# Turning mixed attention values in 32x32 blocks on the vector engine, in a two-layer transformer kernel

## The reference

```python
attn = jax.nn.softmax(jnp.einsum('bnhd,bmhd->bhnm', q, k) * SCALE, axis=-1)
sa = jnp.einsum('bhnm,bmhd->bnhd', attn, v).reshape(Bx, Nx, C)
sa = sa @ sa_proj_w + sa_proj_b
```

## Time and profile before

| | |
|---|---|
| three runs | 1625.62, 1627.46, 1627.52 us (median 1627.46) |
| profiled execution, first to last instruction (the only time the profile gives for it) | 1627.8 us |
| PE, PEld busy | 91%, 79% |
| DVE busy | 69% |
| ACT, POOL busy | 59%, 44% |
| mean DMA rate | 30 GB/s |
| granted clock of PE, mean | 0.978 of full |

### The profile page before, as it was taken

One profiled execution on the slowest core, in us unless ns is written; L12 is line 12 of the kernel. 1 busy time (PEld: TensorE's weight loads), 2 busy tenths in 40 slices (PEclk: granted clock), 3 DMA queues, 4 the chain that ended last, 5 costly groups with the idle time before them and its releaser, 6 DMA issues.

```text
span 1627.8 us, 44574 instructions
## 1 busy us (share of the span) xinstructions
PE 1478.1 (91%) x17632; PEld 1288.7 (79%) x17632; DVE 1130.2 (69%) x2407; ACT 957.0 (59%) x1754; POOL 721.2 (44%) x982
## 2 busy tenths in 40 slices
PE   5989999999999999999998989889899897988987
PEld 4768888787888878788787877878778786887867
DVE  5556766666776766667777776866867777687664
ACT  3456565656656565666655655556655565655543
POOL 3133424333342434336557464464644636356321
PEclk9989999999999999999999999999999999999998
DMA  6110100101010010110112000000000001000000
GB/s 221 45 47 10 37 25 29 41 13 56 10 47 15 29 41 29 40 31 24 36 45 66 12 18 15 14 28 11 18 15 15 27 12 31 5 11 15 2 14 14
DMA packets 34251, 49.38 MB, mean 30 GB/s; under 512 B 3488, under 2 KB 24928, under 8 KB 34048
## 3 DMA queue, kind: packets, MB, share of 16 engines
q1 hardware_dynamic: 33760, 46.01, 9.0%
q10 hardware_dynamic: 288, 0.52, 0.1%
HBM read 38.08 MB, written 8.45 MB: 29 GB/s over the span
## 4 chain that ended last, share of the span: by engine, by line
PE 70%; DVE 16%; issue 7%; ACT 4%; POOL 2%; SPq 0%; DMA 0%; DVEq 0%; POOLq 0%; ACTq 0%
PE score_t L677 8%; PE score L656 8%; PE p_mix L719 7%; PE p_unit L746 6%; PE p_unit L550 5%; PE p_unit L551 5%; PE p_unit L552 5%; DVE neg_max L1120 4%; PE p_out L550 3%; PE p_out L552 3%; PE p_out L551 3%; PE p_mix L581 2%; DVE k_t L1110 2%; PE p_turn L736 2%; PE p_turn L729 2%
## 5 line engine op out<-in xcount | busy, mean ns | idle before, releaser
L1120 DVE TENSOR_REDUCE neg_max<-score 128x8 f32<-128x1024 f32 x224 | 274.1, 1224 | 121.0 <-PE score L656 105.5
L656 PE MATMUL score<-k_t,q_t 32*128 32x256 f32 x1792 | 252.3, 398 | 32.5 <-DVE q_less L1130 16.5
L677 PE MATMUL score_t<-q_less,k_t 32*128 32x128 f32 x3584 | 267.0, 288 | 1.0 <-ACT probs_t L980 0.7
L677 PEld LDWEIGHTS score_t<-q_less,k_t 32*128 32x128 f32 x3584 | 224.0, 191 | 13.1 <-issue 7.1
L980 ACT ACTIVATE probs_t<-score_t 128x1024 f32<-128x1024 f32 x168 | 172.1, 1025 | 94.3 <-PE score_t L677 82.3
L656 PEld LDWEIGHTS score<-k_t,q_t 32*128 32x128 f32 x1792 | 161.5, 186 | 70.3 <-issue 31.6
L899 ACT ACTIVATE xt<-p_mix,mod_now 128x128 f32<-128x128 f32 x384 | 154.4, 454 | 80.3 <-PE p_mix L581 61.5
L1324 POOL TENSOR_TENSOR xt_lo<-xt,xt_hi 128x256 fp32r<-128x256 f32 x128 | 95.8, 749 | 207.1 <-ACT xt_hi L904 206.3
L746 PE MATMUL p_unit<-w_out,heads_t 128*128 128x256 f32 x512 | 147.0, 410 | 15.0 <-ACT q_t L943 8.2
L550 PE MATMUL p_out<-w_hi,hid_lo 128*128 128x256 f32 x512 | 151.9, 297 | 5.0 <-issue 2.6
L1167 DVE TENSOR_TENSOR hid_lo<-hid,hid_hi 128x256 fp32r<-128x256 f32 x256 | 141.8, 554 | 8.8
(11 more groups left out here) (161 smaller groups left out, 4349.1 us busy)
## 6 DMA issues: line engine op xcount, KB each, us to landing
ctxt<-in_ctxT SPq DMA_DIRECT2D x16, 512.0 KB, 3.8
side<-gates SPq DMA_DIRECT2D x15, 512.0 KB, 4.6
x_new<-in_x SPq DMA_DIRECT2D x32, 128.0 KB, 2.1
x_mid<-xs SPq DMA_DIRECT2D x8, 512.0 KB, 3.3
x_new<-x_mid SPq DMA_DIRECT2D x32, 128.0 KB, 2.0
out<-xs SPq DMA_DIRECT2D x8, 512.0 KB, 3.2
k_t<-in_L_f_wT SPq DMA_DIRECT2D x2, 1024.0 KB, 5.6
probs_t<-in_L_xcond_fc_w SPq DMA_DIRECT2D x1, 1024.0 KB, 8.8
```

What stands on the lines that cost most here:

```text
L656: mm = pe.matmul(score_banks(b, h)[:, r % 2, t * 2 * N:(t + 1) * 2 * N].rearrange("p (e n) -> p e n", e=2), q_t[s][rows(r), t, tokens], k_ ...
L677: mm = pe.matmul(turned_banks(b, h)[:, r % 2, x * N:(x + 1) * N], k_t[s][rows(r), t, e, tokens], q_less[rows(r), j % 2, t, e, :], start=Tr ...
L1120: dve.tensor_reduce(by_half[:, 2 * h:2 * h + 2, 0:CT, :], score_banks(b, h)[:].rearrange("p r (t e n) -> p r t e n", t=CT, e=2), AX.X, ALU ...
```

## The change

The matmuls of mix_values write their 128 tokens as four runs of 32 columns into p_mix, so that p_mix holds, for each 32 tokens, the four slots side by side (mix_by_slot). DVE transposes p_mix in 32x32 blocks into SBUF (mix_blocks), takes the reciprocal there, scales out of SBUF into head_blocks, and transposes those in blocks into heads_t. turn_heads, turn_back, move_mix and move_heads and their semaphores go. turn_blocks (transpose and reciprocal) stands in step 7, right behind scale_heads in DVE's order; scale_heads (product and second transpose) in step 8. The release of p_mix, mix_moved, now comes from DVE in step 7, where it came from ACT in step 6. The turned maxima have the former bank p_turn to themselves as p_max; the products of the start that used p_turn now use p_out, and three waits on banks go. The weights and biases of the projection are ordered on the host by row instead of by slot. ACT's order loses two entries, PE's two.

```diff
-AT_TURN_MAX, AT_EXP, AT_MIX, AT_TURN_Q, AT_TURN_BACK, AT_PROJ, AT_STATS, AT_Z, AT_LNT = 2, 3, 6, 7, 8, 9, 10, 11, 11
+AT_TURN_MAX, AT_EXP, AT_MIX, AT_BLOCKS, AT_HEADS, AT_PROJ, AT_STATS, AT_Z, AT_LNT = 2, 3, 6, 7, 8, 9, 10, 11, 11
-PE_ORDER = ("round", "proj", "max", "norm", "mlp", "first", "back", "turn", "unit", "mix")
+PE_ORDER = ("round", "proj", "max", "norm", "mlp", "first", "unit", "mix")
...
+        mix_by_slot = p_mix[:].rearrange("p (c q e i) -> p c e q i", c=CT, q=N // 32, e=2)
...
-                if j == GB:
-                    pe.wait_ge(heads_moved, group * 8 + GB)
-                elif j == GB + 2:
-                    if group:
-                        pe.wait_ge(out_moved, group * 4)
-                    else:
-                        pe.wait_ge(mod_step, 10)
-                pe.transpose(max_bank(j)[:, 0:P], neg_max[:, j % 2, :], ident[:]).then_inc(max_turned, 1)
+                pe.transpose(p_max[:, 0:P], neg_max[:, j % 2, :], ident[:]).then_inc(max_turned, 1)
...
-                        mm = pe.matmul(p_mix[rows(r), x * N:(x + 1) * N], v_pad[s][:, b, at:at + 32],
-                                       probs_t[j % 2][:, r, x, :], start=True, stop=True, tile_position=(0, 32 * r))
+                        mm = pe.matmul(mix_by_slot[rows(r), x // 2, x % 2], v_pad[s][:, b, at:at + 32],
+                                       probs_t[j % 2][:, r, x, :].rearrange("p (q i) -> p q i", i=32),
+                                       start=True, stop=True, tile_position=(0, 32 * r))
...
-            def turn_heads(group, j):
...
-            def turn_back(group, j):
...
-            def move_mix(group, j):
...
-            def move_heads(group, j):
...
+            def turn_blocks(group, j):
+
+                dve.wait_ge(mixed, group * 8 + j + 1)
+                if not (group == 0 and j == 0):
+                    dve.wait_ge(heads_made, group * 8 + j)
+                dve.transpose(mix_blocks[:], p_mix[:]).then_inc(mix_moved, 1)
+                dve.wait_ge(mix_moved, group * 8 + j + 1)
+                dve.reciprocal(rden[:], mix_blocks[:].rearrange("p (h w) -> p h w", h=H)[:, :, HD]).then_inc(rden_made, 1)
+
             def scale_heads(group, j):
-                dve.wait_ge(turned_q, group * 8 + j + 1)
-                by_head = p_turn[:].rearrange("p (h w) -> p h w", h=H)
-                dve.reciprocal(rden[:], by_head[:, :, HD]).then_inc(rden_made, 1)
                 dve.wait_ge(rden_made, group * 8 + j + 1)
                 if not (group == 0 and j == 0):
-                    dve.wait_ge(turned_back, group * 8 + j)
-                dve.tensor_tensor(heads[:].rearrange("p (h d) -> p h d", h=H), by_head[:, :, 0:HD],
+                    dve.wait_ge(heads_moved, group * 8 + j)
+                dve.tensor_tensor(head_blocks[:].rearrange("p (h d) -> p h d", h=H),
+                                  mix_blocks[:].rearrange("p (h w) -> p h w", h=H)[:, :, 0:HD],
                                   rden[:].unsqueeze(2).broadcast_to([P, H, HD]), ALU.mult).then_inc(heads_made, 1)
+                dve.wait_ge(heads_made, group * 8 + j + 1)
+                if not (group == 0 and j == 0):
+                    dve.wait_ge(projected, group * 8 + j)
+                dve.transpose(heads_t[:].rearrange("p t n -> p (t n)"), head_blocks[:]).then_inc(heads_moved, 1)
...
                     for group, step in live(t):
-                        for s, b in batch_at(step, AT_TURN_Q + DVE_SCALE):
+                        for s, b in batch_at(step, AT_HEADS):
                             scale_heads(group, 4 * s + b)
+                    for group, step in live(t):
+                        for s, b in batch_at(step, AT_BLOCKS):
+                            turn_blocks(group, 4 * s + b)
```

More of the change, by code:

```diff
@@ L166 @@
                   + [(FIRST_LNT + b, PLACE["first"], "norm", b) for b in range(GB)])
-TURN_BANK = sorted([(at + AT_TURN_Q, PLACE["turn"], "turn", 4 * s + b) for s, b, at in BATCHES]
-                   + [(at + AT_TURN_BACK, PLACE["back"], "back", 4 * s + b) for s, b, at in BATCHES])
 UNIT_BANK = [sorted([(at + AT_PROJ, PLACE["proj"], "proj", 4 * s + b) for s, b, at in BATCHES]
@@ L293, in build_blocks @@
         p_mix = bank("p_mix")
-        p_turn = bank("p_turn")
+        p_max = bank("p_max")
         p_unit = bank("p_unit")
         p_out = bank("p_out")
+        mix_by_slot = p_mix[:].rearrange("p (c q e i) -> p c e q i", c=CT, q=N // 32, e=2)
         up_ring = [score_t[:, 0], score_t[:, 1], score[:, 0], score[:, 1]]
@@ L567, in bank_free @@
                     pe.wait_ge(ln_moved[m // GB], (group + d) * 4 + m % GB + 1)
-                elif stage == "turn":
-                    pe.wait_ge(heads_made, (group + d) * 8 + m + 1)
-                elif stage == "back":
-                    pe.wait_ge(heads_moved, (group + d) * 8 + m + 1)
                 elif stage == "proj":
@@ L718, in mix_values @@
                         at = VW * (4 * x + r)
-                        mm = pe.matmul(p_mix[rows(r), x * N:(x + 1) * N], v_pad[s][:, b, at:at + 32],
-                                       probs_t[j % 2][:, r, x, :], start=True, stop=True, tile_position=(0, 32 * r))
+                        mm = pe.matmul(mix_by_slot[rows(r), x // 2, x % 2], v_pad[s][:, b, at:at + 32],
+                                       probs_t[j % 2][:, r, x, :].rearrange("p (q i) -> p q i", i=32),
+                                       start=True, stop=True, tile_position=(0, 32 * r))
                 mm.then_inc(mixed, 1)
-            def turn_heads(group, j):
-                pe.wait_ge(mix_moved, group * 8 + j + 1)
-                if group == 0 and j == 0:
-                    pe.wait_ge(bias_added, 1)
-                bank_free(group, around(group, TURN_BANK), "turn", j)
-                for x in range(SLOTS):
-                    mm = pe.transpose(p_turn[:, x * P:(x + 1) * P], mix_sb[:, x * P:(x + 1) * P], ident[:])
-                mm.then_inc(turned_q, 1)
-            def turn_back(group, j):
-                pe.wait_ge(heads_made, group * 8 + j + 1)
-                bank_free(group, around(group, TURN_BANK), "back", j)
-                for c in range(CT):
-                    mm = pe.transpose(p_turn[:, c * P:(c + 1) * P], heads[:, c * P:(c + 1) * P], ident[:])
-                mm.then_inc(turned_back, 1)
             def project(group, s, b):
@@ L771, in down @@
                 half, f = divmod(u, FT)
-                if u == 0:
-                    pe.wait_ge(queries_less[1], (group + 1) * 8 + (4 if group < GROUPS - 1 else 0))
                 if u == 0 and group == 0:
@@ L822, in body @@
                             turn_z(group, 0, b)
-                    for group, step in live(t):
-                        for s, b in batch_at(step, AT_TURN_BACK):
-                            turn_back(group, 4 * s + b)
-                    for group, step in live(t):
-                        for s, b in batch_at(step, AT_TURN_Q):
-                            turn_heads(group, 4 * s + b)
                     for group, step in live(t):
@@ L981, in exps @@
                 op.then_inc(exps_made, 1)
-            def move_mix(group, j):
-                act.wait_ge(mixed, group * 8 + j + 1)
-                if not (group == 0 and j == 0):
-                    act.wait_ge(turned_q, group * 8 + j)
-                act.copy(mix_sb[:], p_mix[:]).then_inc(mix_moved, 1)
-            def move_heads(group, j):
-                act.wait_ge(turned_back, group * 8 + j + 1)
-                if not (group == 0 and j == 0):
-                    act.wait_ge(projected, group * 8 + j)
-                act.copy(heads_t[:].rearrange("p t n -> p (t n)"), p_turn[:, 0:D]).then_inc(heads_moved, 1)
             def split_ctx(group):
@@ L1033, in body @@
                     for group, step in live(t):
-                        for s, b in batch_at(step, AT_TURN_BACK + ACT_HI):
-                            move_heads(group, 4 * s + b)
-                    for group, step in live(t):
                         if step == PRIME_GELU:
@@ L1046, in body @@
                             move_unit(group, UNITS.index(UNIT_AT[layer_of(group)][step - ACT_UNIT]))
-                    for group, step in live(t):
-                        for s, b in batch_at(step, AT_MIX + ACT_MIX):
-                            move_mix(group, 4 * s + b)
             ada_w = a["L0_xcond_ada_w"].rearrange("(t p) n -> t p n", p=P)
```

28 lines of the change are left out of this document (12 added, 16 removed).

## The result

The changed kernel takes 1658.73 us (median of four runs, 1657.88 to 1660.78) against 1627.47: a ratio of 1.0206 with a 95% interval of 1.0194 to 1.0218, slower by some 31 to 33 us where 4 to 5 were forecast.

The account below looks back on a forecast made before the run. PE was taken to pace the kernel, with DVE pacing it in gapless stretches. From 1627.8 us, layer 0 +7, layer 1 +3, fill and drain -6 gave 1631.8, said as 1632; range 1594 to 1660.

Parts of the forecast that it names:

- later release of p_mix: p_mix comes free one transpose later; in steps 7 and 13 within 0.1 us of z: 0, without that cover +0.7 each.
- Durations: DVE's block transposes take 0.72 us for 512 elements and 0.45 for 256; DVE goes from 1130 to about 1277 us.
- rival C: Block transpose is slow, at the upper end 1.5 and 0.75 us: 1697 us, halfway 1665; 12%.
- Rival D: The scattered writes of mix_values are slower: 0.1 us lost per batch would be +13 us; 4%.
- PE sheds: Six transposes per batch leave PE, holding up 0.66 us a batch, 84 us in all.
- rival B: PE's saving stands because DVE's waits absorb turn_blocks in steps 7 and 11: 1580, half standing 1604, value 1592; 32%.
- Steps 23 to 4: Layer 0: of some 2 us that PE gains, none is left at step 4: +0.0, bounds -1 to +0.5.
- Step 7: Layer 0: turn_blocks stands before the keys in gapless DVE work, so PE's unit starts later: +0.6 us.
- Steps 8 to 14: Layer 0: small PE gains against project of step 13 moving +0.6 to +1.5; net of the period about +0.6 us.
- Port: The product, now with both operands in SBUF, contends with POOL's residual add: +0.3 us a period.
- Layer 1: Its periods: net +0.1 and +0.3 for the port, times 8 = +3 us, bounds -8 to +12.
- Fill and drain: Program's start and end: DVE is free with one group live; drain gives 4.5 us, fill 1.5: -6.

Follow-up runs that it names:

- norms_own_bank: Changed kernel with maxima back in the shared bank and turned norms 1 and 2 moved out of the mix's bank: 1646.8 us, 1.0125 of the kernel before.
- pe_part_alone: Kernel before without PE's six transpositions per batch, no transposes put on DVE, the product reading mix_sb: 1604.0 us, ratio 0.9873.

## Why the prediction was wrong

The direction and the mechanism were forecast, DVE's gapless stretches taking back what PE gave; the size was 1632 and is 1659. Two terms of the sum failed. Layer 0 was to cost +0.9 us a period, +7 in all: it cost 1.9 at full clock and 21.6 in seven periods, mostly because the later projection of step 13 and the later release of p_mix, put at nothing net, cost 1.5 us a period in steps 8 to 18. And the end was to give 4.5 us, since DVE "is free" there: it lost 4.9. Behind both stands a price that no term had, that of PE's clock. Step by step:

- **Durations: right.** 0.711 and 0.445 us for the transpositions (forecast 0.72 and 0.45), DVE 1272 (1277). The shuffle was the right neighbour. From 256 to 512 elements the time grows by 266 ns, 1.04 ns per element, so rival C is out. The Trainium skill, "Vector Engine (DVE) Microarchitecture Reference", section 3.8, has one element per cycle and lane for this front end; the rows show one constant time per element, and the length of a cycle stands in none of them. Rival D is out too: the timeline's 32 matmul records of a batch's mix take 1.08 us in both kernels.
- **PE sheds 84 us: too much as work, and wrong as money.** In a full-clock period of layer 0 PE's busy time fell by 3.9 us, not by 5.3, and over the whole run by 45. Taken out of the kernel before, with 30 us of new work on DVE, the transpositions were worth 21 us, without it some 35 by estimate. That is what rival B at 32% had for the saving net of all that DVE adds; but B had DVE's waits absorb the additions, and they cost some 0.47 us per us.
- **Steps 23 to 4, +0.0: right**, the stretches give 0.02.
- **Step 7, +0.6: right**, steps 6 to 8 lose 0.48, by the wait for k_t (0.68 at 627.22) that the prediction named.
- **Steps 8 to 14: the step that failed in the waits.** PE's gains in steps 8 to 14 were to balance a later projection of step 13. They did not: the stretch of steps 8 to 18 lost 1.53 us. The prediction counted one path through DVE (the keys before project) and set "later release of p_mix" to 0, because the norm would see it within 0.1 us of z. In truth it is 1.31 us in step 11, where z stood directly in front of the transposition and the norm had to wait for both, 0.51 in step 13 and 0.74 in step 1. The run norms_own_bank puts the bank's part at 8 to 10 us. The +0.7 that the text gave as the price without the cover was near in size for the steps 13 and 1, and half of that of step 11.
- **Port, +0.3 a period: right in size, by another pair.** The product's group went from 54.4 to 62.6 us, 8.2 / 16 = 0.5 a period. The minimum, median and maximum of one:

```profile
L1089 DVE TENSOR_TENSOR head_blocks<-mix_blocks,rden x128: 409/417/2579, 56.8 to 1620.2; 128x256 f32<-128x256 f32 x128
```

  In layer 0 only the product of step 24 is slow (0.88 us), beside POOL's split of the context; the four next to the residual add, on which the +0.3 was built, are not. The Trainium skill, "SBUF — State Buffer", section "Who interferes with whom", has such pairs block each other for up to an instruction. The rows agree that it happens: PSUM operands never took over 0.426 us. How often depends on what POOL does at that moment: here the median is 417 ns, and in pe_part_alone, where the same product starts at other moments, six of eight in a period of layer 0 are slow, 3.1 us of it.
- **Layer 1, +3 for 8 periods: short by some 5.** The wait for less_max behind the key masks was named and is there (25.5 us in front of score_t). The seven periods gave +7.8, with more time at the lower clock in them, and with the waits filled they are 2.3 us shorter than before. So this loss goes with the clock.
- **Fill and drain, -6: wrong.** The fill gave -3.3 (forecast -1.5), but 2.6 of that lies before the first turned maximum and is not shown to come from the change. The end gave +4.9 in place of -4.5. The clock (0.90 for 0.94) is the smaller part of it: from the last group's turned maximum of step 24 on, the program takes 49.5 us before, 53.1 after, and 53.2 with the waits filled. The prediction had DVE free there. PE's waits for it in the end went from 11.4 to 14.6 us: turn_back's 3.2 are gone, but 1.3 more for z and new ones for the transposition (1.6), heads_t (1.2), the output add (1.2) and hidden units (1.0 more) have come.
- **The clock: the term that was missing.** The prediction treated a wait as costing its own length. PE's gaps grew by 76 us, and with them its time at 1.2 GHz from 72 to 146 us, in which the work that is left takes longer. Filling the waits brings back 8 to 12 us, 6 to 9 of them part of the 31 to 33 by the estimate above. The rows of before gave no clean hint: of its periods of layer 1 the one of the earlier trace rows took 98.79 us at full clock and those at 0.97 over 101, but with the waits filled the periods at full clock reach from 99.4 to 101.9.

So of the loss, 6 to 9 us are the lowered clock (an estimate) and 8 to 10 us are the bank. The rest, about half, has no run of its own; in layer 0 the waits that show it stand behind DVE's list in the steps 2, 3, 7 and 13, and 3.6 us of it lie in the drain. These shares overlap, since a run that shortens waits lifts the clock too (norms_own_bank has 128 us at 1.2 GHz, not 146), and the runs don't split them finer.

## What to carry to other kernels

When two engines share the pace, a move of work is priced by what an us is worth on each: take some out of either alone and look, and check in the trace that the other's busy time stayed as it was. Here it was about 0.4 on PE, in part by estimate, and 0.46 to 0.48 on DVE, so 84 against 142 had to lose. When a release of a buffer moves to another engine, look for that engine's whole list in front of it in every step where the buffer is wanted, not for the one operation. And count new waits of PE twice, once as time and once for the clock that they may cost the work behind them.

## What was not expected of the hardware

- Work added to PE made the kernel faster: 52 more transpositions in a period of layer 0 and 79 in one of layer 1, PE busy 1504 instead of 1433 us, mean granted clock 0.986 instead of 0.956, 8 to 12 us less.
- Periods of layer 0 of the changed kernel, with the same instructions, take 95.85 us at full clock and 97.09 with a mean of 0.97. In layer 1 such periods also differ by up to 2.5 us at full clock, so there the clock's part can't be read from single periods.
- The same product with both operands in SBUF has a median of 417 ns in one kernel and 530 in another (maxima 2579 and 2303), by what POOL does beside it.
- A block transposition takes the same time from PSUM (711 ns) as from SBUF (707 ns) for 512 elements.
